# Unit 0's operand rows in four pieces, loads of 24 outer rows, scores on their own rows only, row maxima turned by one transpose, and a new table of places

## Time and profile before

| what | value |
| --- | --- |
| median of 3 runs | 1024.85 us (1021.96 to 1026.3) |
| span of the profiled execution, first to last instruction | 1017.9 us |
| lowest of the runs less that span | 4.1 us; median less that span 6.95 us |
| TensorE busy, share of the span | 914.7 us, 90% |
| VectorE, ScalarE, GpSimd busy | 716.2, 536.3, 349.8 us |
| mean granted TensorE clock | 0.947 of full speed |
| first exponential | 88.27 us |

### The profile page before, as it was taken

The page is one execution under the profiler, slowest core; times in us unless marked ns, Lnnn a source line. Parts: engine busy times, 40 slices in busy tenths (PEclk is TensorE's granted clock), DMA queues, the critical chain, the costliest instruction groups (busy, mean ns, idle before and its releaser), DMA issues.

```text
span 1017.9 us, 12955 instructions
## 1 busy us (share of the span) xinstructions
PE 914.7 (90%) x4228; PEld 328.1 (32%) x4308; DVE 716.2 (70%) x1344; ACT 536.3 (53%) x1062; POOL 349.8 (34%) x669
## 2 busy tenths in 40 slices
PE   2179988999999999999999999999989999999967
PEld 1022223433433333333322323223233433433333
DVE  6579868768768666865867878778777688683227
ACT  1003755547537545653667666666754367367421
POOL 7521503453253334234330320505124422422423
PEclk9556988999999999999999999999998999999979
DMA  5322220210001001000111031120301200000000
GB/s 166 102 80 56 71 61 24 79 30 1 34 13 47 33 8 51 11 27 7 50 42 43 23 96 22 63 67 30 100 2 67 63 13 3 1 13 3 1 10 10
DMA packets 21733, 41.28 MB, mean 41 GB/s; under 512 B 3308, under 2 KB 19500, under 8 KB 20012
## 3 DMA queue, kind: packets, MB, share of 16 engines
q1 hardware_dynamic: 21428, 40.37, 14.1%
q10 hardware_dynamic: 240, 0.10, 0.0%
HBM read 28.01 MB, written 9.50 MB: 37 GB/s over the span
## 4 chain that ended last, share of the span: by engine, by line
PE 67%; DMA 9%; DVE 8%; issue 6%; POOL 5%; ACT 4%; SPq 1%; POOLq 0%; ACTq 0%; DVEq 0%
PE ps_max L552 14%; PE ps_out L587 14%; PE ps_exp L574 12%; PE ps L648 9%; PE ps L633 5%; DMA qk_parts<-parts 4%; DMA max_parts_rows<-maxT 3%; DVE maxes L726 2%; ACT probs L884 2%; PE ps L599 2%; DVE src L755 2%; PE ps L534 2%; PE ps L611 1%; PE ps L640 1%; PE ps_max L648 1%
## 5 line engine op out<-in xcount | busy, mean ns | idle before, releaser
L884 ACT ACTIVATE probs<-ps_exp 128x512 f32<-128x512 f32 x768 | 434.6, 594 | 298.4 <-PE ps_exp L574 247.4
L726 DVE TENSOR_REDUCE maxes<-ps_max 128x1 f32<-128x512 f32 x768 | 494.3, 684 | 132.0 <-PE ps_max L552 130.3
L552 PE MATMUL ps_max<-k_aug,q_aug 72*128 72x512 bf16 (+1 forms) x768 | 306.3, 401 | 25.8 <-DMA k_aug<-ones_row 12.5
L574 PE MATMUL ps_exp<-q_aug,k_aug 128*128 128x512 bf16 x688 | 265.7, 389 | 16.3 <-DMA q_aug<-max_parts_rows 9.2
L587 PE MATMUL ps_out<-probs,v_aug 128*9 128x512 f32 x1536 | 204.2, 604 | 4.0 <-ACT probs L884 2.2
L552 PEld LDWEIGHTS ps_max<-k_aug,q_aug 72*128 72x128 bf16 (+1 forms) x768 | 74.7, 98 | 265.9 <-DVE maxes L726 141.9
L574 PEld LDWEIGHTS ps_exp<-q_aug,k_aug 128*128 128x128 bf16 x768 | 74.9, 98 | 181.8 <-ACT probs L884 91.9
L648 PE MATMUL ps<-w,hidden 128*128 128x512 f32 x216 | 101.8, 599 | 0.0
L815 DVE TENSOR_TENSOR prod<-ps,gate 128x512 f32<-128x512 f32 x52 | 36.0, 692 | 55.3 <-PE ps L648 43.4
L1078 POOL TENSOR_TENSOR prod<-prod 128x512 f32<-128x512 f32 x28 | 35.5, 1268 | 97.7 <-DVE prod L815 83.0
L963 POOL TENSOR_SCALAR var_eps<-mean_var 128x4 f32<-128x4 f32 x12 | 2.8, 233 | 162.0 <-DVE mean_var L686 162.0
(11 more groups left out here) (165 smaller groups left out, 821.3 us busy)
## 6 DMA issues: line engine op xcount, KB each, us to landing
q_aug<-qk_parts SPq DMA_DIRECT2D x24, 384.0 KB
k_aug<-qk_parts SPq DMA_DIRECT2D x24, 384.0 KB
qk_parts<-parts SPq DMA_DIRECT2D x48, 128.0 KB, 2.3
q_aug<-qk_parts SPq DMA_DIRECT2D x12, 192.0 KB
k_aug<-qk_parts SPq DMA_DIRECT2D x12, 192.0 KB
k_aug<-k_aug SPq DMA_DIRECT2D x4, 576.0 KB
qk_parts<-parts SPq DMA_DIRECT2D x24, 64.0 KB, 2.0
X<-in_x_dram SPq DMA_DIRECT2D x4, 256.0 KB, 4.1
```

The source lines that it names most:

```text
L552: pe.matmul(ps_max[:, n % MAX_RING, :], q_aug[0:k, r, h, qt * 128:(qt + 1) * 128], k_aug[0:k, r, h, :], start=True, stop=True).then_inc(ma ...
L574: pe.matmul(ps_exp[:, n % EXP_RING, :], k_aug[:, r, h, kt * 128:(kt + 1) * 128], q_aug[:, r, h, :], start=True, stop=True).then_inc(exp_fu ...
L726: dve.tensor_reduce(maxes[:, u % 2, h // HH, qt, h % HH:h % HH + 1], ps_max[:, n % MAX_RING, :], AX.X, ALU.max).then_inc(max_done, 1)
L884: act.activation(probs[:, step % P_RING, c, :], ps_exp[:, n % EXP_RING, :], ACT.Exp, scale=scale).then_inc(exp_done, 1)
```

## The change

- **Rows and loads.** In device memory the parts of q lie part by channel by head, those of k channel by part by head. q comes by one DMA for all 72 (36) rows, with 24 (12) outer rows each written three times. k comes by three DMAs of 24 (12) outer rows.
- **Unit 0 in four pieces.** Its loads are issued four heads at a time, each piece with a semaphore of its own: 4 DMAs for q, 16 for k and the ones. The first maximum of a piece waits for that piece alone.
- **No clearing.** The exponentials' matmuls read 75 rows in an ffn unit and 39 in an attn unit (`k = product_rows(u) + PARTS`) in place of 128. The clears, their semaphore and the zeroing DMA are gone.
- **Maxima to rows.** Units 0 and 1 do it in quarters, the others in halves as before. `max_parts` has query tile, part and head side by side, so one transpose gives 96 x 128 (48 x 128 for a quarter) in place of four of 24 x 128. The store then writes runs of 256 bytes in place of 1 KB.
- **Places.** Tile m of unit u stands at `max_place`: unit 0's maxima start 25 places ahead of its exponentials, unit 1's 28, unit 2's 37, the later ones' 42 to 49. Unit 1's preparation and its stack move from before unit 0's exponentials into them (`PREP_SECOND`). All tables are new.

```
-PREP = {"norm_stats": [5], "norm_apply": [7], "x_transpose": [10], "qk_project": [14, 26], "qk_split": [19, 27],
-        "v_project": [16], "stack": [26, 44]}
-PREP_SECOND = {"norm_stats": [0], "norm_apply": [10], "x_transpose": [13], "qk_project": [13, 30],
-               "qk_split": [26, 43], "v_project": [27], "stack": [28, 62]}
-PREP_ATTN = {"norm_stats": [5], "norm_apply": [7], "x_transpose": [11], "qk_project": [14, 26], "qk_split": [22, 40],
-             "v_project": [15], "stack": [26, 56]}
+PREP = {"norm_stats": [0], "norm_apply": [10], "x_transpose": [13], "qk_project": [19, 35], "qk_split": [24, 44],
+        "v_project": [23], "stack": [37, 60]}
+PREP_SECOND = {"norm_stats": [34], "norm_apply": [49], "x_transpose": [53], "qk_project": [55, 72],
+               "qk_split": [62, 80], "v_project": [68], "stack": [84, 89]}
+PREP_THIRD = {"norm_stats": [16], "norm_apply": [23], "x_transpose": [26], "qk_project": [27, 38],
+              "qk_split": [30, 60], "v_project": [35], "stack": [57, 63]}
+PREP_ATTN = {"norm_stats": [4], "norm_apply": [7], "x_transpose": [11], "qk_project": [14, 27], "qk_split": [16, 45],
+             "v_project": [15], "stack": [22, 52]}
...
-MAX_LATE = 15
-ROWS_LATE = [5, 5]
+MAX_LATE = [39, 36, 27, 18, 19, 17, 22, 16, 17, 15, 18, 18, 22]
+ROWS_LATE = 5
...
+def max_place(u, m):
+
+    start, end = ((v - 1) * TILES + MAX_LATE[v] for v in (u, u + 1))
+    return start + m * (end - start) // TILES
...
+                    p0, pieces = product_rows(u), stack_pieces(u)
+                    n = H // pieces
+                    for i in range(pieces):
+                        landed = aug_loaded[r] if u else first_loaded[i]
+                        heads_i = slice(i * n, (i + 1) * n)
+                        of = scratch_rows(u, qk)[:, :, heads_i, :]
+                        if qk == 0:
+                            of = of.rearrange("c d h n -> (c d) h n").unsqueeze(1)
+                            sp.dma_start(q_aug[0:p0, r, heads_i, :], of.to_broadcast([PARTS * d, PARTS, n, S]))\
+                              .then_inc(landed, 16)
+                        else:
+                            for s in range(PARTS):
+                                sp.dma_start(k_aug[PARTS * d * s:PARTS * d * (s + 1), r, heads_i, :],
+                                             of.rearrange("d c h n -> (d c) h n")).then_inc(landed, 16)
+                            sp.dma_start(k_aug[p0:p0 + PARTS, r, heads_i, :],
+                                         ones_row[:, :, :].to_broadcast([PARTS, n, S])).then_inc(landed, 16)
...
-                    pe.matmul(ps_exp[:, n % EXP_RING, :], k_aug[:, r, h, kt * 128:(kt + 1) * 128],
-                              q_aug[:, r, h, :], start=True, stop=True).then_inc(exp_full, 1)
+                    k = product_rows(u) + PARTS
+                    pe.matmul(ps_exp[:, n % EXP_RING, :], k_aug[0:k, r, h, kt * 128:(kt + 1) * 128],
+                              q_aug[0:k, r, h, :], start=True, stop=True).then_inc(exp_full, 1)
...
-                    o = bank(use[0]).bitcast(BF16)
-                    for t in range(TT):
-                        mm = pe.transpose(o[0:PARTS * HH, t * 128:(t + 1) * 128],
-                                          max_parts[:, t, :, :].rearrange("p c h -> p (c h)"), identb[:, :])
-                    mm.then_inc(bank_full[use[0][0]], 1)
+                    n = TT * PARTS * piece_heads(u, i)[1]
+                    pe.transpose(bank(use[0]).bitcast(BF16)[0:n, 0:128], max_parts[:, 0:n], identb[:, :])\
+                      .then_inc(bank_full[use[0][0]], 1)
```

More of the change, by code:

```diff
@@ L53 @@
 P_RING = 2
+PIECES = 4
+STACK_DMAS = 1 + PARTS + 1
+EARLY_UNITS = {0, 1}
 def is_ffn(u):
@@ L76, in product_rows, with stack_pieces, max_pieces, piece_heads @@
     return head_dim(u) * PARTS * PARTS
-def stack_dmas(u):
-    return 2 * PARTS + 1 + (product_rows(u) < product_rows(0))
+def stack_pieces(u):
+    return PIECES if u == 0 else 1
+def max_pieces(u):
+    return PIECES if u in EARLY_UNITS else 2
+def piece_heads(u, i):
+    n = H // max_pieces(u)
+    return i * n, n
+def piece_of(u, h):
+    return h // (H // max_pieces(u))
+def max_rows_before(u):
+    return sum(max_pieces(v) for v in range(u))
+def slot_uses(u, i):
+    return sum(i < max_pieces(v) for v in range(u))
 class Banks:
@@ L178, in plan @@
     for u in range(UNITS):
-        start = (u - 1) * TILES + MAX_LATE
         for m in range(TILES):
[L181 to L185, removed]
+            put(max_place(u, m), "max_scores", u, m // TT, m % TT)
+        for i in range(max_pieces(u)):
+            end = max_place(u, TILES // max_pieces(u) * (i + 1) - 1)
+            put(end, "max_parts", u, i)
+            put(end + ROWS_LATE, "max_rows", u, i)
         for s in range(TILES // 4):
@@ L200, in plan @@
     out = []
-    max_end = (UNITS - 1) * TILES + MAX_LATE
+    max_end = max_place(UNITS - 1, TILES - 1) + 1
     exp_end = UNITS * TILES
@@ L335, in macaron @@
         maxT_stored = sem("maxT_stored")
-        max_loaded = [sem("max_loaded0"), sem("max_loaded1")]
+        first_loaded = [sem(f"first_loaded{i}") for i in range(PIECES)]
+        max_loaded = [sem(f"max_loaded{i}") for i in range(PIECES)]
         exp_full = sem("exp_full")
@@ L385, in stacked, with scratch_rows @@
         def stacked(engine, u):
-            engine.wait_ge(aug_loaded[u % AUG_RING], 16 * sum(stack_dmas(v) for v in range(u % AUG_RING, u + 1, AUG_RING)))
+            if u == 0:
+                for i in range(PIECES):
+                    engine.wait_ge(first_loaded[i], 16 * STACK_DMAS)
+            else:
+                n = sum(1 for v in range(u % AUG_RING, u + 1, AUG_RING) if v)
+                engine.wait_ge(aug_loaded[u % AUG_RING], 16 * STACK_DMAS * n)
+        def scratch_rows(u, qk):
+            d = head_dim(u)
+            v = scratch[u % 2, qk, 0:PARTS * H * d * S]
+            if qk:
+                return v.rearrange("(d c h n) -> d c h n", d=d, c=PARTS, h=H)
+            return v.rearrange("(c d h n) -> c d h n", d=d, c=PARTS, h=H)
         def taken(engine, *step):
@@ new lines, in _ @@
+                    n = H // pieces
[7 more added lines that the diff above has]
+                              .then_inc(landed, 16)
+                        else:
+                            for s in range(PARTS):
[3 more added lines that the diff above has]
+                                         ones_row[:, :, :].to_broadcast([PARTS, n, S])).then_inc(landed, 16)
+                elif name == "max_rows":
+                    i, = args
+                    taken(sp, "max_rows", u, i)
+                    h0, n = piece_heads(u, i)
+                    rows_i = scratch_max[i, 0:PARTS * n * S]
+                    if slot_uses(u, i):
+                        sp.wait_ge(max_loaded[i], 16 * slot_uses(u, i))
+                    sp.dma_start(rows_i.rearrange("(c t q) -> t c q", t=TT, q=128), maxT[0:TT * PARTS * n, :])\
+                        .then_inc(maxT_stored, 16)
+                    sp.wait_ge(maxT_stored, 16 * (max_rows_before(u) + i + 1))
```

122 lines of the change are left out of this document (47 added, 75 removed).

## The result

The changed kernel is faster by 2.7%, where 7.1% was forecast: 998.73 us median of four executions against 1025.14 in the same comparison, ratio 0.9731, interval 0.9689 to 0.9774. The median lies outside the forecast range (938 to 982). One of its four executions took 1082.49 us at a mean TensorE clock of 0.829, and the ratio leaves it out, though the median of 998.73 doesn't; the others took 991.35, 1001.55 and 995.92 at 0.918, 0.909 and 0.915. The profile is of the first: span 989.5 us in 991.35, so 1.85 us lie around the span.

A forecast was written before the change was run, and what follows sets the result against it. TensorE was taken to bound all stretches, the path to unit 0's rows and VectorE's maxima the time before. From span 1017.9, -37.3 +0.8 -6.3 -28.6 -2.5 +0.3 = -73.6 gave 944.3, median 951.3, said as 952; range 938 to 982.

The forecast's parts named there:

- first exponential: Start of unit 0's exponentials: without clears and with faster q loads, near 51 us (48 to 56), -37.3 us.
- unit 0: Its stretch: more maxima +2.4, late k stack of unit 1 +2.5, old wait of 4.1 gone; 58.0 us, +0.8.
- units 1, 2, 9: Their stretches: new places keep GpSimd out of the way of `rms_apply1`; -6.3 us together.
- units 5 and 6: Attn stretches: no places of mixed kinds among maxima and exponentials, so 56.0 us each.
- median over span: Whole kernel: the median lies 6.95 us above the span, taking 944.3 to 951.3.
- the one for units 3 to 8: Their stretches: fewer mixed-kind places and two waits gone, 399.0 us against 427.6, -28.6.
- the 2.5 for the transposes: Maxima to rows: one transpose for four saves 5 us, of which half counts, -2.5 us.
- The rows don't pay: Rival: in units 4, 5, 6 weight loads can't go ahead, 22 us back, 974 us; 12 in 100.
- Waits come back: Rival: waits at the units' starts, 5 us in each of four or five, 972 us; 18 in 100.
- the bounds of 147 and 300: Unit 0's load of q: its rate lies between 147 and 300 GB/s, so it takes 8 to 4 us.
- The 256-byte store: Store of the maxima's rows: bounded below by the old one's 1.4 us and above by twice that.

The follow-up runs named there:

- the base run: The changed kernel with both score matmuls of attn units on 64 rows, not 36 and 39 (attn results not the reference's): 953.17 us.
- the whole kernel on 72 and 75 rows: The changed kernel with attn maxima on 72 rows and exponentials on 75, added k_aug rows zeroed, everything computed: 930.63 us, ratio 0.9109 to the kernel before.

## Why the prediction was wrong

Against the changed kernel's profile, step by step:

| step | forecast | measured |
| --- | --- | --- |
| first exponential | 51 | 54.6 |
| unit 0 | 58.0 | 64.5 |
| units 1, 2, 9 | 84.1, 81.4, 80.8 | 82.7, 80.1, 77.8 |
| units 3, 4 | 88.4, 80.8 | 88.8, 82.2 |
| units 5 and 6 | 112.0 | 154.7 |
| units 7, 8 | 61.8, 56.0 | 61.0, 54.4 |
| unit 10 to the end | 192.5 less part of 2.5 | 188.7 |
| median over span | 6.95 | 1.85 in the profiled execution, whose time is the shortest of four |

**The step that failed** is the one for units 3 to 8, -28.6 us. It priced units 5 and 6 at 56.0 each, and with that took it, without saying so, that TensorE keeps its full clock when all score matmuls use 36 or 39 rows. The profile before had the clock at 1.00 there with exponentials on 128, and I carried that over. The term came out at +13.5: 441.1 against 427.6. With 64 rows in place of 36 and 39, and nothing else, the span is 948.1, 3.8 from the forecast's 944.3. So 41.4 of the 45.2 us between forecast and measured span are this one mechanism, shown by that run, by the steady runs on 72 and 75 rows, and by the kernel before, which becomes 1.5% slower with the rows alone. That the rest is so small is partly luck: in the changed kernel the first exponential and unit 0 are 10.1 us over the forecast, and units 1, 2, 7, 8, 9 and the end are 11.9 us under it (with nothing of the 2.5 for the transposes taken off them).

**No rival had it.** "The rows don't pay" was the nearest and is refuted: start to start is 0.22 us between 39 and 36 rows. Units 4, 7 and 8 came within 1.6 us. "Waits come back" holds for unit 0 only, its wait for k of 4.1 us and the 6.8 us of half clock behind it; that term was mis-sized by 6.5 us (+7.3, not the forecast +0.8, of which +2.5 was for this wait).

**Sizes.** The first exponential is 3.6 us late, and the delay is there when k's stores land, at 31.0, not 27. The stores of q landed in 4.13 us, so the load of q goes out at 21.49, not 20. Its four issues hold SyncE's queue for 3.4 us ahead of k's stores, which the forecast left out, and the last of these goes out at 26.17, not 23.6. It lands in 4.80 us, where the forecast had 3.4. The rate over these stores and the load of q, 203 GB/s, lies inside the bounds of 147 and 300; the 5 us that I took for the 1.18 MB of the load are 236 GB/s. The share is 0.69, as 11 of 16 engines. The Trainium skill (DMA: Bandwidth & Descriptors, Why a DMA increments its semaphore by 16 and not by 1) gives 12 for the new shape, and the trace is near that. Undoing the load's form cost far more than the 9 to 17 us expected of that run: 62.6 us, most of it through later waits and the clock. The 256-byte store landed in 1.9 us (50.35 to 52.24) against 1.4, inside the bounds. The clears cost 3.9 at the first exponential, not 5.9, by a run that clears less than the kernel before did. Unit 9 gained more than forecast (7.8 us, not 4.8) and for a reason other than the one I gave. The 6.95 us that took the forecast from span to median compared different executions: in the same execution the kernel before lies 1.9 us over its span (1023.12 over 1021.2, in a later comparison) and the changed one 1.85.

## What to carry to other kernels

Matmuls on 36 and 39 rows start no closer together than those on 64, or on 72 and 75 (0.22 us for 512 columns in all three), and they can cost the clock. So before narrowing operands, look at the granted clock of the stretch in several executions, and not only at TensorE's busy time: at half the clock it looked busier than ever. Rows filled up with zeros on one side, so that all score matmuls are of one kind, were worth 60.7 us of span here against the changed kernel, since they keep weight loads ahead and the clock up. And a table of places tuned around one transfer's time loses several times that transfer when it gets slower.

## What the runs showed of the hardware that I had not expected

- TensorE went to half its clock while busy for 19.71 of 20 us, with score matmuls on 36 and 39 rows. In the changed kernel this came in unit 5, beside no ffn work; unit 4, beside f32 matmuls on 128 rows, kept 1.00. In the kernel before with exponentials on 39 rows it came in unit 4, so that company doesn't protect. With 64 rows in both kinds of score matmul it held in the base run's four executions of four, with 64 and 39 in three of four.
- Once down it came back late where few rows are used: after 95.6 us in the changed kernel, 30.7 and 37.5 in the kernel before with exponentials on 39 rows, 71.7 in the run with q in three-step loads, 215.0 in the one with exponentials on 75 and maxima on 36 rows.
- How long a wait costs the clock differs as much. Behind a stand of 3.75 us with 64 rows it was down for 71.7 us, behind one of 2.89 us with 36 and 39 rows for 37.5. With 72 and 75 or 128 rows it was 6.8 us behind 3.59 us (the kernel before) and 5.20 us (the whole kernel on 72 and 75 rows), and 10.2 us behind 8.84 us (the same with unit 1's maxima at place 40). In no trace was it over 13.7 us beside score matmuls on 72 rows and more, once unit 0's exponentials were under way.
- Matmuls on 36, 39 and 64 rows are of one kind for the weight load, those on 72, 75 and 128 of another: 0.22 us start to start within a kind, 0.32 across.
